# Two transformer stacks on one core: a new order of the work, one ring of four PSUM banks, weights loaded a layer ahead

## The reference

```python
qkv = x @ Wqkv                                   # 128 -> 3 * 1024
q, k = l2norm(q) * qs, l2norm(k) * ksc           # per head of 64
q = q * cos * scale + rotate_half(q) * sin * scale
k = k * cos * inv + rotate_half(k) * sin * inv
out = local_attention(q, k, v)                   # windows of 32, each sees itself and the one before
x = x + out @ Wo                                 # 1024 -> 128, on shifted tokens
xn = layernorm(x) * g + b
hg = xn @ W1 + b1                                # 128 -> 2 * 341
a, gate = jnp.split(hg, 2, -1)
x = x + (a * gelu(gate)) @ W2 + b2               # 341 -> 128
```

## Time and profile before

| | |
|---|---|
| three runs | 4018.29, 4020.71, 4024.47 us (median 4020.71) |
| profiled execution, own time | 4021.16 us |
| its span in the trace | 4019.4 us |
| granted PE clock, mean | 0.966 |
| busy: PE / DVE / ACT / POOL | 93% / 81% / 61% / 56% |

### The profile page before, as it was taken

The page is one execution under the profiler, slowest core; times in us unless marked ns, Lnnn a source line. Parts: engine busy times, 40 slices in busy tenths (PEclk is TensorE's granted clock), DMA queues, the critical chain, the costliest instruction groups (busy, mean ns, idle before and its releaser), DMA issues. The chain is left out here.

```text
span 4019.4 us, 159581 instructions
## 1 busy us (share of the span) xinstructions
PE 3741.4 (93%) x63216; PEld 2395.6 (60%) x63216; DVE 3244.5 (81%) x11527; ACT 2451.0 (61%) x4337; POOL 2261.0 (56%) x2172
## 2 busy tenths in 40 slices
PE   6899999999999999987698599999999999999997
PEld 3466666666666666652465356666666666666664
DVE  6788888887888888864899688888887888888884
ACT  2467676665767676663422257676666667676674
POOL 1566666665666666643000166666666666666662
PEclk9899999999999999997799699999999999999998
DMA  1222322322323222210000132232322322332221
GB/s 56 76 72 63 79 74 76 84 67 68 82 64 77 75 66 72 72 45 15 1 0 6 33 82 65 71 84 67 79 76 61 80 76 63 81 76 71 70 64 38
DMA packets 170275, 254.12 MB, mean 63 GB/s; under 512 B 36544, under 2 KB 67264, under 8 KB 169408
## 3 DMA queue, kind: packets, MB, share of 16 engines
q1 hardware_dynamic: 169536, 243.87, 23.6%
HBM read 38.21 MB, written 1.05 MB: 10 GB/s over the span
## 5 line engine op out<-in xcount | busy, mean ns | idle before, releaser
L574 PE MATMUL stack_proj<-stack_w_qkv,stack_xs 128*128 128x512 f32 x2304 | 1191.5, 613 | 73.5 <-POOL stack_xs L1205 46.0
L1213 POOL TENSOR_TENSOR stack_roped<-stack_rot_c,stack_rot_s 128x512 f32<-128x512 f32 x768 | 972.9, 1275 | 355.4 <-DVE stack_rot_s L1036 355.4
L1223 POOL TENSOR_TENSOR stack_roped<-stack_roped,stack_rnorm 128x512 f32<-128x512 f32 x768 | 813.1, 1069 | 199.4 <-DVE stack_rnorm L1068 199.4
L1231 POOL TENSOR_TENSOR stack_s_m<-stack_s_m,stack_smax 128x512 f32<-128x512 f32 x384 | 400.6, 1043 | 595.8 <-DVE stack_smax L1079 595.8
L1034 DVE TENSOR_TENSOR stack_rot_c<-stack_proj,rot_tables 128x512 f32<-128x512 f32 x768 | 527.7, 687 | 231.8 <-PE stack_proj L574 225.5
L1079 DVE CUSTOM_DVE_ANT_0 stack_s_m<-stack_bank_s,band 128x64 f32<-128x64 f32 x3072 | 476.1, 220 | 158.4 <-PE stack_bank_s L597 149.7
L574 PEld LDWEIGHTS stack_proj<-stack_w_qkv,stack_xs 128*128 128x128 f32 x2304 | 369.2, 192 | 310.3 <-issue 141.3
L1045 DVE TENSOR_REDUCE stack_ssq<-stack_sq 128x8 f32<-128x512 f32 x768 | 520.5, 678 | 18.3 <-issue 4.3
L873 ACT ACTIVATE stack_sq<-stack_proj 128x512 f32<-128x512 f32 x768 | 460.7, 600 | 110.7 <-DVE stack_rot_s L1036 109.8
L1036 DVE TENSOR_TENSOR stack_rot_s<-stack_proj,rot_tables 128x512 f32<-128x512 f32 x768 | 521.8, 679 | 0.0
L582 PEld LDWEIGHTS stack_turn<-ident,stack_roped 128*128 128x128 f32 x3072 | 362.6, 141 | 224.3 <-issue 204.3
(11 more groups left out here) (256 smaller groups left out, 5227.4 us busy)
## 6 DMA issues: line engine op xcount, KB each, us to landing
stack_v_w<-stack_v_nat SPq DMA_DIRECT2D x1152, 130.0 KB
stack_v_w<-stack_v_nat SPq DMA_DIRECT2D x768, 65.0 KB
stack_w_qkv<-table_ffn_qkv SPq DMA_DIRECT2D x192, 96.0 KB, 2.3
stack_w_o<-table_ffn_wo SPq DMA_DIRECT2D x12, 512.0 KB, 4.7
stack_w<-table_ffn_w SPq DMA_DIRECT2D x12, 384.0 KB, 3.6
stack_w<-table_ffn_w SPq DMA_DIRECT2D x12, 192.0 KB, 3.1
x_outer<-L_attn_a_X SPq DMA_DIRECT2D x4, 256.0 KB, 7.0
ret_xpos<-table_xpos SPq DMA_DIRECT2D x1, 1024.0 KB, 6.4
```

The source lines that it names most:

```text
L574: pe.matmul(bank[:, :], xs[:, T, :], w_qkv[:, g.half, col:col + 512], start=True, stop=True).then_inc(done["proj_" + c], 1)
L1213: pool.tensor_tensor(roped[:, i, T % 2, :], rot_c[:, i % 2, :], rot_s[:, i % 2, :], ALU.add).then_inc(done["roped_" + c], 1)
L1223: pool.tensor_tensor(r, r, rnorm[:, T % 2, i, :].unsqueeze(2).broadcast_to([P, 8, HD]), ALU.mult).then_inc(done["united_" + c], 1)
```

## The change

Four things change in `ffn_stack`; what is computed stays the same.

1. The order in all four engines' `slot` is new. A tile is now spread over six slots of PE (lags 0 to 5, before 0 to 3), and the two score bursts and the first value burst stand next to each other; the second value burst stays apart. The values are projected two slots after the keys and queries. POOL's `stage` for the next tile stands elsewhere in its slot.
2. `proj` and `turnb` become one ring of four banks, `work`, that all of this work goes through in turn. A wait is now for the reader of the piece of work four places back. The bank of each piece is given by the table `BANK`, plus the group's row.
3. `w_o`, `w_1`, `w_2` and `vec` get two halves, and the loads of layer L+1 are issued during layer L.
4. Waits that belong to the new order: `center_out` waits for all six `up` products of the group before, and staging waits for `proj_v0` alone.

```diff
-        w_o = sb("w_o", [P, PAIRS, DIM])
+        w_o = sb("w_o", [P, 2, PAIRS, DIM])
...
-        proj = [ps("proj0"), ps("proj1")]
-        turnb = [ps("turn0"), ps("turn1")]
+        work = [ps(f"work{n}") for n in range(4)]
...
-                    if n == 1 and not first:
-                        sp.wait_ge(done["pe_wo"], 16 * layer + tile0)
-                        apart(sp, layer)
-                        load_wo(layer)
...
+                        if n == 4:
+                            sp.wait_ge(wo_in, 16 * layer + 16 * (layer0 + 1))
+                            apart(sp, layer)
+                            if not first:
+                                sp.wait_ge(done["pe_wo"], 16 * layer + tile0)
+                                apart(sp, layer)
+                            load_wo(layer + 1)
```

PE's slot with T = 2, before and after (the other three differ in which MLP pieces stand in them):

```diff
-                    wait(pe, "squared_q1", N - 1)
-                    up(of(2), "lin", 2, proj[0])
-                    wait(pe, "v_out0", N - 1)
-                    project_out(*at(3), proj[1])
-                    wait_group(pe, "hid2", G - 2)
-                    project(*at(1), "v1", proj[0])
-                    wait(pe, "kept_k1", N - 2)
-                    turn_probs(*at(2), 0, turnb[1])
-                    wait(pe, "mid_set", N - 3)
-                    project(*at(0), "k0", proj[1])
-                    wait(pe, "v_out1", N - 1)
-                    project(*at(0), "q0", proj[0])
-                    wait(pe, "ot_set1", N - 3)
-                    turn(*at(1), "k0", turnb[0])
-                    wait(pe, "normed1", N - 3)
-                    weigh(*at(2), 0)
...
-                    scores(*at(1), 0)
-                    wait(pe, "kept_q1", N - 1)
-                    turn_heads(*at(2), 1, turnb[0])
-                    wait(pe, "squared_k1", N - 0)
-                    project(*at(0), "v0", proj[1])
-                    scores(*at(1), 1)
+                    wait(pe, "squared_k1", N - 1)
+                    turn_heads(*at(5), 0, work[(1 + row) % 4])
+                    wait(pe, "masked1", N - 4)
+                    scores(*at(3), 0)
+                    scores(*at(3), 1)
+                    wait(pe, "normed1", N - 5)
+                    weigh(*at(4), 0)
+                    wait(pe, "squared_q1", N - 1)
+                    turn(*at(2), "q0", work[(2 + row) % 4])
+                    wait_group(pe, "gelu0", G - 2)
+                    turn_probs(*at(4), 1, work[(3 + row) % 4])
+                    wait_group(pe, "gelu2", G - 2)
+                    turn(*at(2), "k0", work[(0 + row) % 4])
+                    wait(pe, "ot_set0", N - 5)
+                    project(*at(0), "k0", work[(1 + row) % 4])
+                    wait(pe, "kept_q0", N - 2)
+                    turn_heads(*at(5), 1, work[(2 + row) % 4])
+                    wait(pe, "pt_set1", N - 4)
+                    project(*at(0), "q0", work[(3 + row) % 4])
+                    wait(pe, "normed0", N - 4)
+                    weigh(*at(4), 1)
+                    wait(pe, "kept_k0", N - 2)
+                    project(*at(2), "v1", work[(0 + row) % 4])
+                    wait(pe, "squared_k0", N - 0)
+                    project_out(*at(5), work[(1 + row) % 4])
+                    wait(pe, "ot_set1", N - 5)
+                    project(*at(2), "v0", work[(2 + row) % 4])
+                    wait(pe, "squared_q0", N - 0)
+                    turn(*at(2), "k1", work[(3 + row) % 4])
+                    wait(pe, "v_out1", N - 2)
+                    turn_probs(*at(3), 0, work[(0 + row) % 4])
+                    wait(pe, "mid_set", N - 5)
+                    turn(*at(2), "q1", work[(1 + row) % 4])
+                    wait(pe, "v_out0", N - 2)
+                    project(*at(0), "k1", work[(2 + row) % 4])
+                    wait(pe, "kept_k1", N - 2)
+                    project(*at(0), "q1", work[(3 + row) % 4])
+                    wait(pe, "pt_set0", N - 3)
+                    up(of(2), "lin", 2, work[(0 + row) % 4])
```

DVE's slot, without the MLP pieces, and POOL's slot after:

```diff
+                mask_max(*at(3), 0)
+                sum_squares(*at(1), "q1")
+                norm_heads(*at(4), 0)
+                rotate(*at(0), "k0")
+                norms(*at(1), 0)
+                rotate(*at(0), "q0")
+                mask_max(*at(3), 1)
+                norm_heads(*at(4), 1)
+                mid(*at(5))
+                norms(*at(1), 1)
+                sum_squares(*at(0), "k0")
+                norms(*at(1), 2)
+                sum_squares(*at(0), "q0")
+                norms(*at(1), 3)
+                rotate(*at(0), "k1")
+                rotate(*at(0), "q1")
+                sum_squares(*at(0), "k1")
...
+                unit(*at(3), "q0")
+                unit(*at(3), "k0")
+                rope(*at(2), "k1")
+                rope(*at(2), "q1")
+                off_max(*at(4), 0)
+                unit(*at(3), "k1")
+                unit(*at(3), "q1")
+                rope(*at(1), "k0")
+                stage(*at(0))
+                off_max(*at(4), 1)
+                rope(*at(1), "q0")
```

More of the change, by code:

```diff
@@ L642, in project_out @@
                 for n in range(PAIRS):
-                    last = pe.matmul(bank[:, 0:P], w_o[:, n, :], o_t[:, T % 2, n, :], start=n == 0, stop=n == PAIRS - 1)
+                    last = pe.matmul(bank[:, 0:P], w_o[:, g.half, n, :], o_t[:, T % 2, n, :], start=n == 0, stop=n == PAIRS - 1)
                 last.then_inc(done["pe_wo"], 1)
@@ L663, in up @@
                 n = min(P, HID - P * k)
-                pe.matmul(bank[0:n, :], w_1[:, 3 * (kind == "lin") + k, 0:n], x_c[:, :], start=True, stop=True
+                pe.matmul(bank[0:n, :], w_1[:, g.half, 3 * (kind == "lin") + k, 0:n], x_c[:, :], start=True, stop=True
                           ).then_inc(done[f"pe_{kind}{k}"], 1)
@@ L848, in _ @@
+                    wait(pe, "pt_set0", N - 3)
+                    project(*at(0), "q1", work[(0 + row) % 4])
             pe.wait_ge(consts_set, N_CONSTS * (run + 1))
@@ L938, in center_square @@
                 wait_group(act, "pe_center", g)
-                act.activation(c_sq[:, :], proj[PROJ["ct"]][:, :], ACT.Square).then_inc(done["center_sq"], 1)
+                act.activation(c_sq[:, :], work[(BANK["ct"] + g.row) % 4][:, :], ACT.Square).then_inc(done["center_sq"], 1)
             def center_out(g):
@@ L944, in center_out @@
                 wait_group(act, "pe_center", g)
-                wait_group(act, "pe_lin2", g.number - 1)
-                act.copy(x_c[:, :], proj[PROJ["ct"]][:, :]).then_inc(done["center_set"], 1)
+                for k in range(3):
+                    wait_group(act, f"pe_gate{k}", g.number - 1)
+                    wait_group(act, f"pe_lin{k}", g.number - 1)
+                act.copy(x_c[:, :], work[(BANK["ct"] + g.row) % 4][:, :]).then_inc(done["center_set"], 1)
             def inv_std(g):
@@ L952, in inv_std @@
                 wait_group(act, "xn_set", g.number - 1)
[L953 removed]
+                act.activation(std[:, :], work[(BANK["va"] + g.row) % 4][:, :], ACT.Ln, bias=eps[:, :]).then_inc(done["std_read"], 1)
                 wait_group(act, "std_read", g)
@@ L1101, in mid @@
                     wait_x(dve, g.number - 2)
-                bank = proj[PROJ["wo"][T]]
+                bank = work[(BANK["wo"][T] + g.row) % 4]
                 for rows, first in ((slice(0, 64), P * T), (slice(64, P), P * T + 1)):
@@ L1128, in finish @@
                 wait_group(dve, "pe_down", g)
-                bank = proj[PROJ["w2"]]
+                bank = work[(BANK["w2"] + g.row) % 4]
                 for rows, first in ((slice(0, 64), 0), (slice(64, P), 1)):
-                    last = dve.scalar_tensor_tensor(xst[rows, g.row, first:first + SEQ], bank[rows, :], vec[rows, 8:9],
+                    last = dve.scalar_tensor_tensor(xst[rows, g.row, first:first + SEQ], bank[rows, :], vec[rows, g.half, 8:9],
                                                     mshift[rows, g.pair, first:first + SEQ], ALU.add, ALU.add)
```

468 lines of the change are left out of this document (213 added, 255 removed).

## The result

The changed kernel is slower: 4190.43 us (median of 4 runs, 4181.26 to 4202.89) against 4021.49 (4018.29 to 4024.47), a ratio of 1.042 with a 95% interval of 1.039 to 1.045. The prediction was 3879 us, faster; it was wrong in sign and by 311 us.

What follows compares the result with a forecast made beforehand. PE, busy 93% of the span, was taken as the bound, with 2.44 us of waits a group. 48 groups x 3.38 = 162 us off 4021.2 and 20 on for the deeper pipeline gave 3879 us, range 3785 to 3970.

Steps and rivals of the forecast that it cites:

- joined burst: Three of a tile's four small-product bursts put together: 2.40 us against 2.37 for three separate ones, +0.12 us a group.
- slower rival: Joined burst starves, up to 25 ns for each of 160 passes: 346 us more, 4225 us; chance 0.08.
- The Trainium skill's queue: 64 entries in front of PE, 62 ns per matmul; joined burst then about 10 us, over 1000 us lost; rejected.
- Borders: PE's extra cost entering and leaving bursts: 2.60 us a group becomes 1.36, saving 1.24.
- Waits: PE's waits inside a stack: 2.44 us a group, among them the staging copy's, fall to 0.2.
- Ring and weights ahead: Four-bank ring costs no instruction and makes the margins; loading weights a layer ahead changes nothing.
- Deeper pipeline: Two slots more at each stack's start and end: 10 us a stack, 20 in all (0 to 32).

Runs made afterwards that it cites:

- the probe: Kernel before plus PE-only bursts of 64, 96, 128 and 192 small products behind each stack, value spreads behind the second; 192 passes took 2.04 us unstalled.
- spaced version: Changed kernel with bursts set apart, first score burst in the slot before, second at the slot's start; the second of two such versions: 3908.9 us, 0.9717 of before.
- first probe: Kernel before plus PE-only bursts of 128 to 768 passes behind each stack, value spreads behind the second; four bursts of 768 passes took 18.3 to 20.2 us.

## Why the prediction was wrong

- **The failed step: the joined burst.** I read from the earlier trace rows that the first half of a burst comes from "work that stood ready", put the rest between two paces, and took 2.40 us for the whole. The pace was right: 2.42 us in the kernel where nothing stops it, 2.04 in the probe. But only 56 of 190 joined bursts ran so; the mean was 3.73 us. What failed is that two paces seen inside 64 passes were taken as all that can happen to 192. A limit of another kind comes in above 128 passes: a whole block of 256 instructions used up in 1.4 us, with about 3.5 us needed for the next. It was not seen in the trace of before, because no stretch there uses a block up so fast: between two single bursts stand at least four transposes and a product, 0.50 and 0.95 us by the earlier trace rows, so that 256 instructions take some 3.0 us (0.79 + 1.45 + 0.79); the fastest 256 in the trace between 400 and 1100 us take 2.8. That is close to the edge, and five stops of up to 0.3 us in the score bursts, 1.1 in all, may be its traces. The average did not warn either: 2591 instructions in 72.7 us are ten blocks, one per 7 us.
- **The slower rival, 0.08, was the case.** It said that the joined burst starves, with 25 ns a pass at worst and a change of sign above 3.14 us. The 768-pass bursts took 25 ns a pass. In the kernel a joined burst took 3.73 us in the mean, and 126 of 190 were over 3.14; the sign's point was well placed, the chance was not. I argued against it with "the second 32 need only 0.52", which is a row on a short burst and says nothing on a long one.
- **Where the error is.** In the profiled executions (4195.9 and 4021.2 us) it is 317 us, in the medians 311. The joined bursts are 190 x (3.73 - 2.40) = 253 of it, 226 of them idle time in or directly behind the burst. Issue idle elsewhere is some 282 - 226 - 15 = 41. The start and end of the stacks cost more than the 20 forecast, by 17 (below). That leaves 6 us, a remainder in which costs that were too high and a lower clock (0.96 to 0.98 in windows of 500 us in the stacks, where before had 0.99 to 1.00) meet; they were not measured apart.
- **The Trainium skill's queue** ("TensorE: Matmul & The Clock Gate", part 1), by which I took 64 entries as the store and rejected 62 ns a pass: no run shows 62 ns. The store that decided is another one. The Trainium skill's page "Runtime: NRT & Kernel Launch", section "Instruction fetch mechanics", states blocks of 16 KiB, 256 instructions, that are fetched while the one before runs. With the blocks the runs agree (stalls multiples of 256 instructions apart, one 16 KB packet for each 256). It also says that crossing a block's end is mostly hidden; here it cost 0.5 to 2.8 us (the stalls of over 0.5 us in the changed kernel) when a block was used up in or around a joined burst.
- **Borders**: not tested apart. In the spaced version the group takes 66.0 us with 16 single bursts, whose borders I priced at 2.60 and whose content at 63.94: 66.5. So the price of borders was high by some 0.5 us at least, or the single costs read to 0.05 were.
- **Waits** 2.44 to 0.2: right. The staging copy is no releaser in the profile after, and all waits of the projections are 21.6 us in the kernel. There the stalls give the other engines extra time, so the second spaced version is the better test: apart from one wait at each stack's end, the largest waits in the stack are for squares, 15 us at each of two lines.
- **Ring and weights ahead** at 0: the weights are shown alone. The ring was not, only together with the depth.
- **Deeper pipeline**, 20 us (0 to 32): first projection to first output projection is 68.7 us (47.3 before; I said 60), and 68.9 and 45.5 in the second stack, +45 in all. The first projection starts 1 us later, and the end of the kernel and the way between the stacks give back 8.5, which leaves 37. In the second spaced version +36 and -7.5: 28 us, inside the range.
- **The spaced version by the same sums**: period 65.6 + 1.24 - 0.12 = 66.7, saved 2.26, with the ramp 3933; measured 3909. The sums of costs and waits come within 24 us there; the one limit that they lacked decided.

## What to carry to other kernels

Small TensorE products are cheap in time and dear in instructions, two for each pass. Before bursts are put together, see that no block of 256 instructions is used up faster than the next can be brought in (about 3.5 us here, a little longer beside other transfers). Neither a low mean rate nor the price of a short burst says anything on that. "Issue" idle in the middle of a burst, at places that move from one repetition to the next and lie multiples of 256 instructions apart, is its sign. The new ring of banks did not prevent it here; other work between the bursts did.

## What the runs showed of the hardware

- PE's instructions come in steps of 256: 142 of 168 distances between stalls in the changed kernel are within 3 of a multiple of it, and the probes added one instruction packet for every 256. A step took 3.4 to 3.7 us where the supply set the pace (14.7 us for four in a long burst; 3.49 us for 260 instructions in the rows with one product between). PE went on 1.2 to 1.8 us after a step's 16 KB had landed (126 of 130 stalls in the changed kernel, 59 of 59 in the first probe). In bursts of 192 passes behind 2.6 us or more of large work, PE stood 1.4 to 2.6 us when a step was used up inside.
- Value spreads under way made the spaced bursts of 128 passes longer by 0.2 us (1.70 to 1.93), the unbroken joined bursts by 0.3 (2.14 to 2.42, clock 1.00 in both), and the changed kernel by 93 us; the kernel before by 5.
- After a stall of 2.0 us the granted clock was 0.50 for a burst's next 128 passes (1.94 us), and 0.70 over the 4 us behind the one at 603.38. Across four stops of 0.55 to 1.03 us between 1943.49 and 1958.84 in the first probe it was 1.00.
- With instructions at hand, bursts of 64, 96, 128 and 192 passes took 0.79, 1.10, 1.42 and 2.04 us: about 9.8 ns for each further pass, and 0.16 us once.
